# Four-layer graph network: one loop for the sort, one stage for two index lists, softmax shares formed ahead of the weighting, and products added up in PSUM

## The reference

```python
x = _layernorm(x + _L0_gnn_ref(...))   # mean over edges of x[col], two matrices, relu
x = _layernorm(x + _L1_gnn_ref(...))   # attention over edges, 4 heads of 32
x = _layernorm(x + _L2_gnn_ref(...))   # weighted sum over edges
x = _layernorm(x + _L3_gnn_ref(...))   # 18 matrices by edge type, both directions
```

```python
kj = k[src] + e
vj = v[src] + e
alpha = jnp.einsum('ehc,ehc->eh', q[dst], kj) / np.sqrt(C)
amax = jax.ops.segment_max(alpha, dst, num_segments=n)
ex = jnp.exp(alpha - amax[dst])
denom = jax.ops.segment_sum(ex, dst, num_segments=n)
alpha = ex / (denom[dst] + 1e-16)
agg = jax.ops.segment_sum(vj * alpha[:, :, None], dst, num_segments=n)
out = agg.reshape(n, HID) + (x @ Wskip + bskip)
```

## Time and profile before

| | us |
|---|---|
| median of three runs | 5444.95 (5442.43 to 5445.99) |
| the profiled execution | 5444.79 |
| its span | 5443.0 |
| POOL busy | 3678.0 (68%) |
| PE busy | 2800.3 (51%) |
| DVE busy | 2380.8 (44%) |
| ACT busy | 486.2 (9%) |

### The profile page before, as it was taken

How to read it: one execution, slowest core, us unless ns; L and a number is a source line. 1 busy time by engine, 2 the same in 40 slices (tenths; PEclk the granted TensorE clock), 3 DMA queues, 4 the chain that set the end, 5 groups by cost and what they waited for, 6 DMA issues and landing times. The chain is left out here.

```text
span 5443.0 us, 56992 instructions
## 1 busy us (share of the span) xinstructions
PE 2800.3 (51%) x13330; PEld 2304.1 (42%) x13331; DVE 2380.8 (44%) x3403; ACT 486.2 (9%) x765; POOL 3678.0 (68%) x3586
## 2 busy tenths in 40 slices
PE   1169999845555555525664873333333333333333
PEld 1158888832333333314554842333333333333332
DVE  6589998623555555556776054111111111111111
ACT  0035555000000000000001000000000000000000
POOL 0068888876777777774442755777777777777775
PEclk9999999867777777767877986555555665555555
DMA  4135555714888888844441843222222222221222
GB/s 128 32 92 135 133 131 138 273 33 109 216 216 220 217 216 219 215 125 114 120 118 50 294 163 110 53 53 53 53 53 53 53 49 53 53 53 53 53 53 53
DMA packets 692133, 626.43 MB, mean 115 GB/s; under 512 B 205815, under 2 KB 592037, under 8 KB 688357
## 3 DMA queue, kind: packets, MB, share of 16 engines
q1 hardware_dynamic: 455461, 294.10, 19.6%
q0 software_dynamic: 118496, 222.54, 16.0%
q10 hardware_dynamic: 118112, 109.05, 6.1%
HBM read 447.90 MB, written 190.20 MB: 117 GB/s over the span
## 5 line engine op out<-in xcount | busy, mean ns | idle before, releaser
L823 PE MATMUL ps<-g_got,g_hot 128*128 128x128 f32 x3264 | 759.3, 427 | 1295.3 <-DMA g_got<-y,s_msg 648.0
L585 POOL DMA_INDIRECT rec_by_src<-rec,pos x782 | 1070.2, 1368 | 431.7 <-issue 244.3
L823 PEld LDWEIGHTS ps<-g_got,g_hot 128*128 128x128 f32 x3264 | 705.2, 328 | 1349.5 <-issue 1349.5
L794 POOL DMA_INDIRECT g_got<-y,d_msg x816 | 769.8, 943 | 259.4 <-issue 248.4
L794 POOL DMA_INDIRECT g_got<-y,s_msg x816 | 769.8, 943 | 257.2 <-issue 248.4
L1091 POOL DMA_INDIRECT sc_kv<-kv,sc_cur x816 | 786.7, 964 | 220.3 <-issue 196.5
L647 PE MATMUL ps<-ln_low,ln_hot 128*125 128x256 f32 x2848 | 617.3, 380 | 11.3 <-DVE ln_low L624 11.3
L647 PEld LDWEIGHTS ps<-ln_low,ln_hot 128*125 128x125 f32 x2848 | 536.4, 188 | 92.1 <-issue 11.5
L807 DVE TENSOR_TENSOR g_hot<-ps,src_loc 128x1024 f32<-128x1024 f32 x102 | 124.5, 1224 | 840.7 <-PE ps L823 840.4
L807 DVE TENSOR_TENSOR g_hot<-ps,dst_loc 128x1024 f32<-128x1024 f32 x102 | 124.5, 1224 | 837.8 <-PE ps L823 837.5
L1142 DVE TENSOR_TENSOR sc_kve<-sc_kv,ps 128x1024 f32<-128x1024 f32 x204 | 249.2, 1221 | 395.7 <-DMA sc_kv<-kv,sc_cur 220.3
(11 more groups left out here) (277 smaller groups left out, 2529.3 us busy)
## 6 DMA issues: line engine op xcount, KB each, us to landing
linked<-ln_out SPq DMA_DIRECT2D x320, 224.0 KB
sc_locb<-loc SPq DMA_DIRECT2D x204, 256.0 KB, 3.7
ve<-sc_kve ACTq DMA_DIRECT2D x204, 256.0 KB, 5.0
wv_ve<-ve SPq DMA_DIRECT2D x102, 512.0 KB, 4.0
l_links<-linked SPq DMA_DIRECT2D x50, 800.0 KB, 6.8
l_links<-linked ACTq DMA_DIRECT2D x50, 800.0 KB, 8.7
y<-ms_y SPq DMA_DIRECT2D x25, 1152.0 KB
sc_attr<-attr SPq DMA_DIRECT2D x816, 16.0 KB
```

Of the source, the lines that this page charges most:

```text
L585: pool.indirect_dma_start(out=dram["rec_by_src"], out_offset=bass.IndirectOffsetOnAxis(ap=S["pos"][:, c:c + 1], axis=0), in_=S["rec"][:, c ...
L794: pool.indirect_dma_start(out=got[:, q, j, :], out_offset=None, in_=table, in_offset=bass.IndirectOffsetOnAxis(ap=index[:, c:c + 1], axis= ...
L823: last = pe.matmul(ps[:, bass.ds(columns[j], width)], hot[:, q, j, :], got[:, q, j, 0:width], start=False, stop=True, skip_group_check=True)
```

## The change

In six parts.

1. `sort_by_block` takes the place of `sort_by_key` for the sort by source (the run-time branch for inputs that are not sorted by destination keeps the old one; here it isn't taken). All 25 masks are made first, each with its count from the same instruction; two products give all first places; then for each block a scan that starts at the first place and a multiply with the mask; PE adds the 25 products in PSUM.
2. `index_stage` takes the place of `staircase`. The windows and the pairs go through one stage: one fetch of the firsts, counts taken by `accum_out` of the comparing instruction, the gathers of both one after the other, then POOL sends 10 tiles of records. src uses it too.
3. `RECORD_PARTS` changes, and sends are counted by one semaphore, which is waited for only behind the last one (in messages).
4. `softmax_maxima` goes on after the exponential: a segmented sum forward, its last value spread backward, and for each head 1e-16 added, a reciprocal and a multiply. What is stored is alpha divided by its sum.
5. `weigh_values` has a ring of six buffers, fetched by SP and ACT in turn. DVE makes hot and multiplies ve in its buffer; PE adds into PSUM at places that its sequencer reads; POOL sends records; the end adds PSUM to skip.
6. `mlp_layer` of m1 has no average any more and reads skip.

```diff
-RECORD_PARTS = {"link": 320, "l0": 105, "m0": 30, "project": 45, "maxima": 60, "l2": 105, "messages": 0}
+RECORD_PARTS = {"index": 10, "link": 300, "l0": 70, "m0": 34, "project": 44, "maxima": 90, "weigh": 110, "m1": 40, "l2": 60, "messages": 0}

+def sort_by_block(nc, S):
...
+            for k in range(BLOCKS):
+                dve.tensor_scalar(mask[:, k, :], key[:, :], float(k), 0.0, ALU.is_equal, ALU.add,
+                                  accum_out=count[:, k:k + 1]).then_inc(counted, 1)
...
+            for k in range(BLOCKS):
+                dve.tensor_tensor_scan(rank[:, k % 2, :], ones[:, :], mask[:, k, :], first[:, k:k + 1], ALU.mult, ALU.add).then_inc(ranked, 1)
+                dve.wait_ge(ranked, k + 1)
+                dve.tensor_tensor(mask[:, k, :], mask[:, k, :], rank[:, k % 2, :], ALU.mult).then_inc(placed, 1)
+            dve.wait_ge(placed, BLOCKS)
+            dve.wait_ge(gathered, 1)
+            link(dve.tensor_copy(S["pos"][:, :], ps[:, 0:TILES]))
...
+            for k in range(BLOCKS):
+                pe.wait_ge(placed, k + 1)
+                for lo in range(0, TILES, BANK):
+                    hi = min(lo + BANK, TILES)
+                    last = pe.matmul(ps[:, lo:hi], S["ident"][:, :], mask[:, k, lo:hi], start=k == 0, stop=k == BLOCKS - 1)

 index_stage (staircase before)
-            for c in range(pair_blocks):
-                link(dve.tensor_scalar(below[:, :], climb[:, :], limit[:, c:c + 1], None, ALU.is_lt))
-                link(dve.tensor_reduce(count[:, c:c + 1], below[:, :], AX.X, ALU.add))
+                for c in range(blocks):
+                    link(dve.tensor_scalar(below[:, :], s.climb[:, :], s.limit[:, c:c + 1], 0.0, ALU.is_lt, ALU.add,
+                                           accum_out=s.count[:, c:c + 1]))
+            for k, s in enumerate(stairs):
+                pool.wait_ge(tiled, k + 1)
+                pool.nop(nofuse=True)
+                for c in range(s.blocks):
+                    pool.indirect_dma_start(out=s.rows[:, c, :], out_offset=None, in_=whole,
+                                            in_offset=bass.IndirectOffsetOnAxis(ap=s.tile_i[:, c:c + 1], axis=0)).then_inc(got[k], 16)
+            if send is not None:
+                send_records(pool, S, dram, send)

 send_records
-                                in_=S["rec"][:, c * REC:(c + 1) * REC], in_offset=None).then_inc(sent, 16)
-    pool.wait_ge(sent, 16 * (last - first))
+                                in_=S["rec"][:, c * REC:(c + 1) * REC], in_offset=None).then_inc(S["sent"], 16)
+    if last == TILES:
+        pool.wait_ge(S["sent"], 16 * TILES)

 softmax_maxima
-                sp.wait_ge(exped, h + 1)
+                sp.wait_ge(shared, h + 1)
+            link(dve.tensor_scalar(stops, anyc[:, 0:1].to_broadcast([P, HEADS]), -1.0, 1.0, ALU.mult, ALU.add))
+            dve.wait_ge(exped, HEADS)
+            carried(2, False, same, score, 0.0, ALU.mult, ALU.add)
+            for h in range(HEADS):
+                link(dve.tensor_tensor_scan(top[:, h, :], same[:, :], score[:, h, :], into[:, h:h + 1], ALU.mult, ALU.add))
+            link(dve.tensor_scalar_mul(stops, anyc[:, 1:2].to_broadcast([P, HEADS]), -BIG))
+            carried(3, True, node_a, top, -BIG, ALU.add, ALU.max)
+            for h in range(HEADS):
...
+                link(dve.tensor_tensor_scan(backward(both[:, :]), backward(node_a[:, :]), backward(top[:, h, :]), into[:, h:h + 1], ALU.add, ALU.max))
+                link(dve.tensor_scalar_add(both[:, :], both[:, :], 1e-16))
+                link(dve.reciprocal(both[:, :], both[:, :]))
+                dve.tensor_tensor(score[:, h, :], score[:, h, :], both[:, :], ALU.mult).then_inc(shared, 1)

 weigh_values
+        def fetch(eng, first):
+            with eng.Fori(0, WHOLE) as i:
+                for q in range(first, WAYS, 2):
+                    eng.wait_ge(summed[q], i + 1)
+                    eng.dma_start(ve[:, q], dram["ve"][bass.ds(start_of(i, q), GROUP), :, :].rearrange("k e d -> e k d")).then_inc(landed[q], 16)
...
+            with dve.Fori(0, WHOLE) as i:
+                for q in range(WAYS):
+                    cols = bass.ds(start_of(i, q), GROUP)
+                    dve.wait_ge(summed[q], i + 1)
+                    dve.tensor_tensor(hot[:, q], iota[:, :].unsqueeze(1).to_broadcast([P, GROUP, P]),
+                                      S["dst_loc"][:, cols].unsqueeze(2).to_broadcast([P, GROUP, P]), ALU.is_equal).then_inc(heated[q], 1)
+                    dve.wait_ge(landed[q], (i + 1) * 16)
+                    ve4 = ve[:, q].rearrange("p k (a c) -> p k a c", c=HEAD)
+                    dve.tensor_tensor(ve4, ve4, S["alpha"][:, :, cols].rearrange("p a k -> p k a")
+                                      .unsqueeze(3).to_broadcast([P, GROUP, HEADS, HEAD]), ALU.mult).then_inc(weighed[q], 1)
...
+            dve.tensor_tensor(S["skip"][:, :], S["skip"][:, :], ps[:, 0:BLOCKS * D], ALU.add).then_inc(added, 1)
...
+                    columns = load_columns(nc, S, mybir.EngineType.PE, "dst", 1, start_of(i, q))
+                    pe.wait_ge(heated[q], i + 1)
+                    pe.wait_ge(weighed[q], i + 1)
+                    for j in range(GROUP):
+                        last = pe.matmul(ps[:, bass.ds(columns[j], D)], hot[:, q, j, :], ve[:, q, j, :],
+                                         start=False, stop=True, skip_group_check=True)
+                    last.then_inc(summed[q], 1)
```

More of the change, by code:

```diff
@@ L404, in staircase, with index_stage @@
+def index_stage(nc, S, dram, tag, node_field, records, specs, send=None):
     with ExitStack() as stack:
         m = Memory(nc, stack)
-        rows = m.sb(name + "_rows", [P, pair_blocks, P * REC])
-        wide = m.sb(name + "_wide", [P, 2, cols])
-        fields = rows[:, :, :].rearrange("p b (e r) -> p b e r", r=REC)
-        nodes = m.sb(name + "_nodes", [P, cols]) if any(what == "node" for _, what in outputs) else None
-        high_i = m.sb(name + "_highi", [P, cols], I32) if windows else None
@@ L480, in _ @@
             link = Chain(dve, order)
-            dve.wait_ge(spread, 1)
-            dve.wait_ge(ready, 4)
-            if windows:
-                link(dve.tensor_scalar_mul(held[:, 0:SPLIT_BLOCKS], split[:, :], float(per)))
-                for c in range(SPLIT_BLOCKS):
-                    link(dve.tensor_scalar(below[:, :], S["ps"][:, 0:TILES], held[:, c:c + 1], None, ALU.is_lt))
-                    link(dve.tensor_reduce(count[:, pair_blocks + c:pair_blocks + c + 1], below[:, :], AX.X, ALU.add))
@@ L555, in _ @@
+            dve.wait_ge(listed, len(stairs))
         @block.tensor
@@ L583, in send_records @@
+def send_records(pool, S, dram, stage):
     first, last = part_of(stage)
@@ L1319, in _ @@
                 link(dve.tensor_copy(into[:, :], ps[:, 5 * BANK:5 * BANK + HEADS]))
-                for h in range(HEADS):
-                    dest = top[:, h, :] if way == 0 else both[:, :]
-                    link(dve.tensor_tensor_scan(run(dest), run(edge[:, :]), run(src[:, h, :]), into[:, h:h + 1], ALU.add, ALU.max))
-                    if way == 1:
-                        link(dve.tensor_tensor(score[:, h, :], score[:, h, :], both[:, :], ALU.subtract))
-                        dve.engine_nop().then_inc(ready, 1)
+            stops = ends[:, HEADS:2 * HEADS]
@@ new lines, in _ @@
+            for h in range(HEADS):
+                if h:
+                    dve.wait_ge(shared, h)
+                link(dve.tensor_tensor_scan(backward(both[:, :]), backward(node_a[:, :]), backward(top[:, h, :]), into[:, h:h + 1], ALU.add, ALU.max))
+                link(dve.tensor_scalar_add(both[:, :], both[:, :], 1e-16))
+                link(dve.reciprocal(both[:, :], both[:, :]))
+                dve.tensor_tensor(score[:, h, :], score[:, h, :], both[:, :], ALU.mult).then_inc(shared, 1)
@@ L1362, in _ @@
[L1362 to L1369 removed]
+            send_records(pool, S, dram, "weigh")
         @block.vector
```

524 lines of the change are left out of this document (269 added, 255 removed).

## The result

The changed kernel takes 5084.66 us, the median of four runs (5081.84 to 5085.49); the kernel before took 5445.47 beside it. The ratio is 0.9337, 95% interval 0.9321 to 0.9353. Forecast were 5108 us, in a range of 5070 to 5205. The profiled execution has a span of 5082.6 us, 360.4 less than before; so the forecast of -336.5 was 24 too small.

A forecast was written before the change was run, and what follows sets the result against it. Most stages were taken as bound by chains of hand-overs, not a full engine; stage times add. Terms -62 -46 -4 -7.5 -50 +71 -210 -12 -16 = -336.5 from 5444.8 gave 5108 us, range 5070 to 5205.

The forecast's parts named there:

- Sort: Sort by source: 25 masks with counts, then scans and multiplies with PE hidden, 102 us for 164: -62 (-72 to -47).
- Index: Index stages: windows and pairs in one stage, counts at 1.07, earlier gathers, end at 272 instead of 318: -46 (-54 to -36).
- Link: Link stage: DVE stays full; 20 sends less and no landing wait, so the table's stores end it: -7.5 (0 to -15).
- l0: l0 stage: 70 sends for 105, so POOL ends 44 us earlier, and no landing wait: -50 (-54 to -44).
- nothing is waited for: Step for l0: with POOL done at 1129.6 and DVE at 1127.7, the stage ends at 1134 at most instead of 1183.9.
- Softmax: Softmax stage grows by mask, carries, scans and four reciprocals of 6.3 us over 816 elements: +71 (+50 to +76).
- Rival C: Softmax: a cheap reciprocal, 4 x 5.3 = 21 us less, total 5087; chance 5%.
- Weigh: Weigh stage: DVE sets each of 102 groups at 2.4 us instead of 4.6, stage 259: -210 (-221 to -70).
- Rival A: Weigh: PE's clock stays at the half, a group takes 3.78 us, total 5249; chance 5%.
- Rival B: Weigh: ring fed too slowly or sequencer waits adding up on PE, 3.0 to 3.3 a group, total 5169 to 5200; chance 12%.
- the rival of one buffer: Weigh: the six-buffer ring acts as one buffer, 7.2 us a group, total 5597, slower than before; chance 2%.
- Rival E: Softmax, weigh or m1: POOL fails to catch up with its sends and ends those stages, total 5168; chance 8%.

The follow-up runs named there:

- e11: Changed kernel with the old sort, and windows and pairs in two index stages, each with the new counting: 5187.12 us, ratio 0.9526.
- e2: Changed kernel with the old send numbers (none in weigh) and POOL waiting for landing at each stage's end: 5931.92 us, ratio 0.9529, on a slower chip.
- e3: Changed kernel with the old send numbers (none in weigh) and one wait behind the last send alone: 5937.81 us, ratio 0.9531, on a slower chip.
- e6: Changed kernel with logarithm and exponential for the reciprocal, and sends l0 62, maxima 70, weigh 103, l2 95: 5054.34 us, ratio 0.9279.
- e8: Changed kernel with logarithm and exponential for the reciprocal, weigh's multiply on POOL, and sends redistributed (l0 62, weigh 0): 5024.02 us, ratio 0.9225.
- e5: Changed kernel with ScalarE's logarithm and exponential for the softmax reciprocal, 70 sends there and 80 in l2: 5062.4 us, ratio 0.9294.
- e10: Changed kernel with two buffers in weigh instead of six, one on each queue: 5306.8 us, ratio 0.9746, weigh 467.1 us.
- e7: Changed kernel with weigh's multiply on POOL instead of VectorE and no sends there (l2 110, messages 84): 5043.16 us, ratio 0.926.

## Why the prediction was right, and where its sizes were off

**Sort (-62, measured -69).** Mechanism as put: no wait for PE, two wide operations less in the loop. The term "25 masks at 1.07" was mis-sized: 0.89, since in the sort no mask waits for the one before it; in the index stage, where each count waits for the last, they do follow every 1.07 (140.59, 141.67). That is 4.5 of the 7 us. Scan and multiply at 2.77 for 2.84 are 1.8 more. PE's products were hidden, as said, from the third block on at the full clock.

**Index (-46, measured -43).** As put; e11 parts it. The windows' first gather came 26.1 after the stage's start, the forecast had 24.3. Where the rest of the 3 us went was not looked for.

**Link (-7.5, measured -16).** The mechanism as put, the size at its bound. Before, SP was through with the table's stores at 954.4 and POOL's DRAIN at 969.4; now POOL is through at 827.8 and SP at 842.2, so the stores end the stage, 15 earlier. The sum had booked half of that without a reason.

**l0 (-50, measured -51).** The number was right and a part of the reason wrong. The step "nothing is waited for" failed: the barrier still waits for POOL's DRAIN. With 35 sends fewer the last one ended 46 us earlier, and wait and drain behind it took 5.8 us where they had taken 9.9. POOL's row in the changed kernel ends at 984.2 + 21.0 = 1005.2, and VectorE was done at 1000.3 (the second DRAIN is that of l2):

```profile
L773 POOLq DRAIN  x2: 21017/21942/22867, 984.2 to 2722.8; - x2
```

The prediction read the 10 us behind the last send as waiting for the landing. e2 and e3 show that this wait is worth 1.2 to 1.4 us; the rest was the DRAIN. The sum came out because the DRAIN is shorter behind fewer sends, and that is luck. With 62 sends the stage is 2 to 4 us shorter (e6, e8).

**Softmax (+71, measured +66).** The reciprocal over 816 elements took 5.25 us. I had taken the slope of the last two rows, 7.6 ns an element; measured are 5.25 / 816 = 6.4 ns. That is 4.2 of the 5 us. Two rows 5 elements apart were too near for a slope. The trace of before had a third:

```profile
L892 DVE RECIPROCAL m_den<-m_den x5: 190/191/191, 1184.1 to 1219.6; 128x5 f32<-128x5 f32 x5
```

From 5 to 25 elements it gives (316 - 191) / 20 = 6.25 ns, and 316 + 791 x 6.25 = 5260 ns for 816, which is what was measured. The rule of the Trainium skill (page "VectorE: DVE Perf Modes", First, the fixed hardware budget), eight steps an element, gives 6.8 us by estimate and is off by 1.6. Rival C, a cheap reciprocal at 1.0, is refuted too; what can be gained with ScalarE in its place is 21.5 (e5).

**Weigh (-210, measured -218).** VectorE sets the group, at 2.28 and not 2.4, 12 us less than forecast, and the first hot came 3 us after the stage's start and not 8; the low end of the range, 2.3 from link's pace, was the better guess. 8 us come back as POOL's drain, which the sum did not have, though it had reckoned POOL's sends as "hidden" by 41 us. That was wrong: at 2.26 a send in the loop, in step with VectorE, 110 sends last as long as the loop. Rival A (half clock) did not come: 0.97 with PE busy 84%. The Trainium skill's rule (page "TensorE: Matmul & The Clock Gate", What's actually happening), that the slow clock is the default and activity lifts it, goes with 0.97 here and 0.59 in the ring of one. Rival B (ring fed too slowly) did not come with six buffers; with two it is all there, and the rival of one buffer was slower than before, at 9.5 us a group where I had priced 7.2 (with the products at the full clock).

One reason in the text was too weak. The prediction booked weigh's gain to what leaves VectorE, and gave the ring a sentence. e10 shows that without the ring nothing is gained: with two buffers a group takes 4.6 us in both divisions of work that were measured. The other half, the ring without the moves, was not run; the gain needs both, as far as VectorE's 335 us tell. And e7 shows that VectorE needn't multiply at all.

**Rival E (the sends only move)** came true in one of its three stages. In weigh the slower sends used up the 41 us to spare, and POOL's drain ended the stage, by 8 us; softmax and m1 POOL did not end. It also ended l0, by 5, which no rival had.

**m1, messages, src, l2**: -11, -17, -4 and 0 for -12, -16, -4 and 0; as put.

Of the signs named ahead, the one for the reciprocal (rows of 6 to 7 us) failed at 5.25. g3 and g4, "nearly half of the time" in the prediction, are 2077 of 5443 us, 38%; nothing in the sum hangs on it.

## What to carry to other kernels

Where a loop hands a buffer round through fetch, multiply and product, first divide the time of one turn of a buffer by the number of buffers: only when that is below the slowest engine's share does moving work between engines gain anything. Behind a stage's last indirect DMA on GpSimd, count the DRAIN until the barrier opens, waited for or not: here 2.8 us with 34 sends, 5.8 with 70 and 9.0 with 110. Give each stage so few that they are through before the others. Where two engines are free beside a full one, ask what each would take for the same operation beside its other work: here POOL's slower multiply was the faster kernel.
